# An attention kernel's projections: pieces and their evictions set by a table for each body

## The chip, the cores and the metric

The kernel runs on one core of one Trainium2 chip. The time is that of one launch on the device, in microseconds (us); of several runs the median is given. The core has a matrix engine (TensorE, PE in the rows), VectorE (DVE), ScalarE (ACT), GpSimd (POOL) and SyncE (SP, which here issues transfers). Each runs its own list of instructions in order, and waits at semaphores for the others.

## The reference: what is computed

`x` has 8 images of 56 by 56 cells with 256 channels, in float32. The block is attention between windows, behind a group norm:

```python
x = x + L0_conv_ref(gn(x), ...)            # gn: 32 groups of 8 channels
# inside:
qkv = einsum('nchw,oc->nohw', xc, qkv_w) + qkv_b
q_r, k_r = pool(q), pool(k)                # means over 7 x 7 regions of 8 x 8 cells
_, idx_r = top_k(q_r @ k_r, 4)             # for each region: the 4 regions to look at
attn = softmax(einsum('bhnqd,bhnkd->bhnqk', qs * SCALE, key_g))   # 64 queries, 256 keys, 8 heads
out = einsum('bhnqk,bhnkd->bhnqd', attn, val_g)
out = out + conv3x3_depthwise(v) + lepe_b
out = einsum('nchw,oc->nohw', out, out_w) + out_b
```

So each of the 8 x 49 regions gathers the keys and values of 4 regions of its image, and beside that there are four projections (q, k, v, output) and a 3 x 3 convolution for each channel.

## The kernel before

**Tiles.** A row is a band of 8 lines of cells: 448 cells and 7 regions, and 7 rows make an image, so there are 56 rows. Channels lie on the 128 partitions in two halves, so a projection of one row has two *chunks*, `v0` and `v1`, `k0` and `k1`, and so on, each 128 by 448 in one of two PSUM banks (`chunk_bank`), which the chunks take in turn. A chunk is 4 *pieces*: two halves of 224 cells, each over two halves of the channels. `vt0` and `vt1` turn the values of a row over (one piece each), `rm` makes the means of the regions of an image, and `late` is half of an output projection that is kept for the last image.

**Bodies.** The program is unrolled into some 200 bodies, each for two regions (a *duo*); one body in each image but the last has a single region. With 25 bodies to an image I number them 0 to 24; body 0 is the single one, which ends the image before. In body h TensorE does the scores of duo h (`scores`, L1218), the product of probabilities and values of duo h-1 (`attend`, L1258), turns the reciprocals of the softmax sums (`turn_recips`, L1266), and then four times: some pieces of projections (`fill`), and the turn of two heads' worth of probabilities for each of the two regions (`turn_probs`, L1240, turns 0 to 3). The pieces fill the time in which TensorE would otherwise wait for the softmax.

**The softmax's loop.** The scores of a duo need all exponentials of the one before (they share banks). VectorE takes the maximum of each turn (L959, four instructions), ScalarE the exponential (`exp`, L744, two heads and their sums for each region), and ScalarE copies each turned bank out (`probs_t_out`, L754). There are two buffers of probabilities: the exponentials of turn 2 need turn 0 done, and those of turn 3 turn 1.

**Evictions.** ScalarE takes v, k, q, vt and rm chunks out of their bank (L701, L691, L720, L711, L729); VectorE takes output chunks, adding the input (`out_half`, L944; `late_half`). A chunk can't begin before the chunk two before it is out of the bank. VectorE also does the convolution (`outer_tap`, L846, 16 a row) and the statistics of later rows, in `row_part`, once for each region (*slot*).

**What sets the order.** `step_order` lists the chunks of each row; this list is the same before and after. `fill_plan` cuts it into bodies by weights: a piece weighs 2, a turn of values 3, a piece of `rm` 1; the four fills of a body get about 4, 5, 4 and what is left up to the goal of the slot. Chunks ended in fills 0 and 1 go out on ScalarE behind the exponentials of turn 2, those ended in fills 2 and 3 at the start of the next body, the first of them ahead of the last copy of probabilities and the others behind it. On VectorE an output chunk goes out ahead of the first slot's part (fill 0), between the two slots (fills 1 and 2), or at the start of the next body, ahead of the maxima (fill 3).

**Transfers.** SyncE stores the turned values of each row (`store_values`) and gathers them for each region in four transfers (`select_values`, L441) into 4 slots (`v_sel`); it reads the indices of 7 regions at a time (L404). GpSimd gathers keys, adds the attention's result to the convolution, and issues the transfers of whole rows.

## Time and profile before

| | us |
|---|---|
| median of 3 runs | 1795.88 (1792.58 to 1802.46) |
| the profiled execution | 1792.81 |
| its span, first to last instruction | 1789.8 |
| busy: TensorE | 1636.2 (91%) |
| busy: VectorE | 1530.6 (86%) |
| busy: ScalarE | 1383.9 (77%) |
| busy: GpSimd | 1052.2 (59%) |

A busy share is a mean over the run. The chain of work that ended last goes 61% over TensorE, 11% over VectorE, 9% over ScalarE, and 10% of it is time between instructions with no wait that shows. The ends of matrix instructions are modelled, so a short wait between two groups of them can be hidden in the busy time; the starts are measured, and from one group's start to the next is what the argument uses. The granted clock was 0.996 of full speed over the run.

### The profile page before, as it was taken

What the parts mean: (1) busy time and instruction counts of PE and PEld (TensorE: products, weight loads), DVE (VectorE), ACT (ScalarE), POOL (GpSimd) and SP (SyncE); (2) the same over time, 40 slices, a digit from 0 to 9 for tenths busy, and PEclk for the clock granted to TensorE, in tenths of its full rate; (3) what the DMA queues carried; (4) which work ended last, traced back from release to release, by engine and by line L of the source; (5) the groups of instructions that cost most, each with busy time, mean ns of one, the idle gap of its engine ahead of it and who ended that gap; (6) DMA issues with size and microseconds to landing.
All of it is one profiled execution on the core that took longest, in us unless ns stands there. A gap on an engine that the chain in (4) does not pass through costs nothing.

```text
span 1789.8 us, 73643 instructions
## 1 busy us (share of the span) xinstructions
PE 1636.2 (91%) x26568; PEld 1377.4 (77%) x26568; DVE 1530.6 (86%) x2951; ACT 1383.9 (77%) x4401; POOL 1052.2 (59%) x2548
## 2 busy tenths in 40 slices
PE   5999999999999899899999999899899999999897
PEld 4877777887778777777777788788787878777676
DVE  6589888899889889888888889899898888889895
ACT  2488778888778788788888788788787888877674
POOL 3256556566566565655565566556556666577664
PEclk9999999999999999999999999999999999999998
DMA  5233434343434343344444444434343334366555
GB/s 200 77 97 120 126 103 139 108 149 117 127 113 137 107 149 115 116 123 122 126 119 129 123 126 121 125 107 151 105 127 102 115 103 129 113 203 196 196 185 191
DMA packets 164632, 234.43 MB, mean 131 GB/s; under 512 B 19232, under 2 KB 146912, under 8 KB 164272
## 3 DMA queue, kind: packets, MB, share of 16 engines
q1 hardware_dynamic: 141408, 129.71, 24.7%
q0 software_dynamic: 22864, 100.02, 16.7%
q8 instruction: 214, 3.51, 0.8%
q14 instruction: 146, 1.20, 0.2%
HBM read 166.80 MB, written 62.85 MB: 128 GB/s over the span
## 4 chain that ended last, share of the span: by engine, by line
PE 61%; DVE 11%; issue 10%; ACT 9%; POOL 4%; DMA 2%; SPq 2%; POOLq 1%; ACTq 0%; DVEq 0%
PE chunk_bank L1124 20%; PE pt_bank L1240 10%; PE s_bank L1218 10%; ACT probs L744 7%; PE o_bank L1258 6%; DVE neg_max L959 5%; PE o_bank L1240 4%; PE chunk_bank L1138 3%; DVE lepe L846 2%; PE o_bank L1266 2%; POOL k_sel L502 2%; PE chunk_bank L1166 2%; PE chunk_bank L1151 1%; POOL lepe L514 1%; DMA v_sel<-v_dram 1%
## 5 line engine op out<-in xcount | busy, mean ns | idle before, releaser
L744 ACT ACTIVATE probs<-s_bank,neg_max 128x256 f32<-128x256 f32 x1568 | 734.0, 483 | 240.7 <-DVE neg_max L959 240.7
L502 POOL COPY k_sel<-k_all 128x128 f32 x1568 | 397.1, 302 | 512.4 <-PE s_bank L1218 421.9
L959 DVE TENSOR_REDUCE neg_max<-s_bank 128x2 f32<-128x512 f32 x784 | 486.8, 682 | 161.2 <-PE s_bank L1218 160.6
L846 DVE SCALAR_TENSOR_TENSOR lepe<-v_band,taps,lepe 128x448 f32<-128x448 f32 x896 | 621.3, 743 | 0.0
L1124 PE MATMUL chunk_bank<-xn,wqkv 128*128 128x224 f32 x2544 | 588.9, 357 | 29.0 <-ACT v_stage L711 13.4
L1124 PEld LDWEIGHTS chunk_bank<-xn,wqkv 128*128 128x128 f32 x2544 | 439.7, 192 | 40.9 <-issue 37.2
L754 ACT COPY probs_t<-pt_bank 128x512 f32<-128x512 f32 x611 | 364.5, 597 | 81.8 <-PE pt_bank L1240 79.3
L1240 PE MATMUL pt_bank<-ident,probs 128*128 128x128 f32 x2444 | 375.9, 276 | 22.4 <-ACT probs L744 13.3
L1240 PEld LDWEIGHTS pt_bank<-ident,probs 128*128 128x128 f32 x2444 | 281.4, 141 | 98.7 <-issue 69.4
L514 POOL TENSOR_TENSOR lepe<-o_norm,lepe 128x128 f32<-128x128 f32 x392 | 263.8, 692 | 150.7 <-DVE o_norm L982 147.3
L744 ACT ACTIVATION_READ_ACCUMULATOR probs<-s_bank,neg_max 128x1 f32 x1568 | 332.1, 212 | 0.0
L1258 PEld LDWEIGHTS o_bank<-probs_t,v_sel 128*32 128x32 f32 x12544 | 186.3, 110 | 103.0 <-issue 96.7
L1258 PE MATMUL o_bank<-probs_t,v_sel 128*32 128x64 f32 x12544 | 221.1, 221 | 23.8 <-issue 18.0
L1218 PE MATMUL s_bank<-k_sel,q_all 32*64 32x256 f32 x6272 | 220.9, 387 | 2.6 <-POOL k_sel L502 2.2
L1138 PE MATMUL chunk_bank<-lepe,wout 128*128 128x224 f32 x696 | 162.1, 355 | 14.0 <-POOL lepe L514 10.2
L1218 PEld LDWEIGHTS s_bank<-k_sel,q_all 32*64 32x64 f32 x6272 | 114.9, 131 | 51.4 <-issue 33.7
L1138 PEld LDWEIGHTS chunk_bank<-lepe,wout 128*128 128x128 f32 x696 | 121.0, 190 | 19.2 <-POOL lepe L514 17.3
L754 ACT COPY probs_t<-o_bank 128x512 f32<-128x512 f32 x173 | 106.3, 614 | 8.1 <-PE o_bank L1240 8.1
L1240 PE MATMUL o_bank<-ident,probs 128*128 128x128 f32 x692 | 103.9, 273 | 0.0
L525 POOL TENSOR_SCALAR lepe<-v_band,taps,btap 128x448 f32<-128x448 f32 x112 | 102.7, 917 | 0.0
L1266 PE MATMUL o_bank<-ident,o_norm 128*128 128x128 f32 x392 | 87.1, 302 | 12.0 <-issue 6.4
L563 POOL TENSOR_SCALAR xn<-xn,rstd,shift 128x448 f32<-128x448 f32 x96 | 93.6, 975 | 0.0
(81 smaller groups left out, 1442.6 us busy)
## 6 DMA issues: line engine op xcount, KB each, us to landing
v_sel<-v_dram SPq DMA_DIRECT2D x1568, 64.0 KB
xn<-x_dram POOLq DMA_DIRECT2D x56, 448.0 KB, 4.9
v_dram<-v_stage SPq DMA_DIRECT2D x112, 224.0 KB
resid<-x_dram POOLq DMA_DIRECT2D x31, 448.0 KB, 4.6
out_dram<-resid POOLq DMA_DIRECT2D x31, 448.0 KB, 5.6
spill<-lepe POOLq DMA_DIRECT2D x25, 448.0 KB, 3.6
xn<-spill POOLq DMA_DIRECT2D x25, 448.0 KB, 5.5
resid<-x_dram POOLq DMA_DIRECT2D x25, 224.0 KB, 3.3
```

The lines of the kernel that those rows point to most:

```text
L502: last = pool.tensor_copy(k_sel[:, r % K_SLOTS, :, RT * j:RT * (j + 1)], k_all[:, b % 2, :, bass.ds(reg[j] * RT, RT)])
L514: pool.tensor_tensor(cells, o_norm[:, r - DUOS[h][0], :].rearrange("p (k r c) -> p k r c", k=KC, r=RS), cells, ALU.add).then_inc(o_row_don ...
L744: act.activation(probs[:, 2 * (j % 2) + i, :], s_bank[:, u, KEYS * at:KEYS * (at + 1)], ACT.Exp, bias=neg_max[:, h % 2, col:col + 1], accu ...
L754: act.copy(probs_t[:, j, :], turn_bank(h, j)[:, :]).then_inc(probs_t_evac, 1)
L846: ins = dve.scalar_tensor_tensor(row, v_band[:, n % BANDS, k, t // 3:t // 3 + RS, t % 3:t % 3 + W], taps[:, k, t:t + 1], row, ALU.mult, AL ...
L959: dve.tensor_reduce(neg_max[:, h % 2, 2 * j:2 * j + 2], scored, AX.X, ALU.max, negate=True).then_inc(max_done, 1)
L1124: ins = pe.matmul(bank_of(kind, n, k)[:, cols], wqkv[:, part, col:col + P], xn[:, part, n % X_RING, cols], start=(part == 0), stop=(part = ...
L1138: ins = pe.matmul(bank_of("out", g, m)[:, cols], wout[:, part, P * m:P * (m + 1)], lepe[:, part, g % LEPE_RING, cols], start=(part == 0), ...
L1218: last = pe.matmul(s_bank[RT * k:RT * (k + 1), u, KEYS * i:KEYS * (i + 1)], q_all[s, g % Q_RING, k, rc, :], k_sel[s, r % K_SLOTS, k, :], s ...
L1240: ins = pe.transpose(bank[:, at:at + P], probs[:, 2 * (j % 2) + i, P * c:P * (c + 1)], ident[:])
L1258: last = pe.matmul(o_bank[HD * u:HD * (u + 1), P * i + RT * k:P * i + RT * (k + 1)], v_sel[:, r % V_SLOTS, c, HD * head:HD * (head + 1)], ...
L1266: last = pe.transpose(o_bank[:, P * (DUO + i):P * (DUO + i + 1)], o_norm[:, i, :], ident[:])
```

## The change: a table of pieces and places

For each body of an image a table now holds four counts, the pieces of the four fills, and two strings of four letters, one for ScalarE and one for VectorE: where in its order the engine takes out a chunk that ended in that fill. On ScalarE, 0 is behind the exponentials of turn 1, 1 behind the copy of turn 0, 2 behind the exponentials of turn 2, 3 behind the copy of turn 1, 4 behind the exponentials of turn 3, 5 behind the copy of turn 2, and W at the start of the next body as before. On VectorE, N is ahead of the first slot's part, H behind it, I between two taps of the second slot's part, E at the body's end, and W at the start of the next body. There is one table for the first image, one for the next six, one for the last. Values are stored two regions later: by SyncE behind the gathers of slot 1 of the next row instead of slot 6 of their own (the last row of an image as before).

```diff
-def quotas(h, slots):
-    if not is_duo(h) or not slots:
-        return [0] * (2 * len(slots))
-    return [4, 5, 4, 0] if len(slots) == DUO else [4, 0]
+NEXT_IMAGES = (
+    "3171 .1WW ....", "1404 .2.4 ....", "2322 .1.5 ..H.", "2223 .3.W ....", "2340 .14. ....",
+    "2513 0..W .H.E", "2241 1.WW ....", "2404 .2.W ....", "2422 1W.. ...E", "0114 .2WW ....",
...
+def body_table(h):
+    if h == 0:
+        return [0] * (2 * len(BODIES[0][1])), "", ""
+    firsts = [DUO_OF[NREG * b] + (b < NB - 1) for b in range(NB)]
+    b = max(b for b in range(NB) if firsts[b] <= h)
+    table = FIRST_IMAGE if b == 0 else NEXT_IMAGES if b < NB - 1 else LAST_IMAGE
+    counts, by_act, by_dve = table[h - firsts[b]].split()
+    return [int(c) for c in counts], by_act, by_dve
...
 def fill_plan():
+        for count in body_table(h)[0]:
             place = []
+            for key, i in stream[at:at + count]:
                 if place and place[-1][0] == key:
                     place[-1] = (key, place[-1][1], i + 1)
                 else:
                     place.append((key, i, i + 1))
             places.append(place)
+            at += count
...
+def taken(h, by_act, at):
+    if not 0 <= h < len(PLAN):
+        return []
+    _, act_at, dve_at = body_table(h)
+    return [key for f, place in enumerate(PLAN[h]) for key, _, last in place
+            if last == pieces(key)[0] and (key[0] not in ("out", "late")) == by_act
+            and (act_at if by_act else dve_at)[f] in at]
...
-                    if rc == 0 and rr == 1 and is_row(kv - 1):
+                    if rc == 1 and rr and is_row(kv - 1):
                         store_values(kv - 1)
                     if rc == 1 and rr == LAST and is_row(kv):
                         load_index(kv // NWIN)
-                    if rc == 6 and rr not in (0, LAST) and is_row(kv):
-                        store_values(kv)
...
             for h, slots in BODIES[1:]:
+                left = taken(h - 1, True, "W")
                 for key in left[:1]:
                     chunk_out(*key)
                 if is_duo(h - 1):
                     probs_t_out(h - 1, turns_of(h - 1) - 1)
                 for key in left[1:]:
                     chunk_out(*key)
+                if is_duo(h):
+                    exp(h, 0)
+                    exp(h, 1)
+                    chunks_out(h, "0")
+                    probs_t_out(h, 0)
+                    chunks_out(h, "1")
+                if is_duo(h) and turns_of(h) > 2:
                     exp(h, 2)
+                    chunks_out(h, "2")
                     probs_t_out(h, 1)
+                    chunks_out(h, "3")
                     exp(h, 3)
+                    chunks_out(h, "4")
                     probs_t_out(h, 2)
+                    chunks_out(h, "5")
...
                 if is_duo(h - 1):
                     normalize_o(h - 1)
+                sums_out(h, "N")
+                if len(slots) == 1:
                     row_part(slots[0])
+                    sums_out(h, "HI")
                 else:
+                    row_part(slots[0])
+                    sums_out(h, "H")
+                    row_part(slots[1], h)
+                    for slot in slots[2:]:
+                        row_part(slot)
+                sums_out(h, "E")
```

The first place is ScalarE's order in body 2 of the second image, from the last copy of probabilities of body 1 on; line numbers of the two kernels differ (L744, L754, L691 and L701 of before are L759, L769, L706 and L716 of after). Before:

```order
L754 COPY probs_t<-pt_bank 128x512
L744 ACTIVATE probs,denom<-s_bank,neg_max 128x256 x4
L754 COPY probs_t<-pt_bank 128x512
L744 ACTIVATE probs,denom<-s_bank,neg_max 128x256 x2
L701 ACTIVATE v_band<-chunk_bank,bqkv 128x8x56
L691 ACTIVATE k_all<-chunk_bank,bqkv 128x8x7x8
L754 COPY probs_t<-pt_bank 128x512
L744 ACTIVATE probs,denom<-s_bank,neg_max 128x256 x2
L754 COPY probs_t<-o_bank 128x512
L691 ACTIVATE k_all<-chunk_bank,bqkv 128x8x7x8
```

And the same stretch after:

```order
L769 COPY probs_t<-pt_bank 128x512
L716 ACTIVATE v_band<-chunk_bank,bqkv 128x8x56
L759 ACTIVATE probs,denom<-s_bank,neg_max 128x256 x4
L769 COPY probs_t<-pt_bank 128x512
L759 ACTIVATE probs,denom<-s_bank,neg_max 128x256 x2
L706 ACTIVATE k_all<-chunk_bank,bqkv 128x8x7x8
L769 COPY probs_t<-pt_bank 128x512
L759 ACTIVATE probs,denom<-s_bank,neg_max 128x256 x2
L706 ACTIVATE k_all<-chunk_bank,bqkv 128x8x7x8
L769 COPY probs_t<-o_bank 128x512
```

The eviction of `v1` has moved out of the stretch between the first and the last exponentials to a place ahead of them, that of `k0` has stayed, and that of `k1` goes ahead of the copy of turn 2.

The second place is TensorE's order in body 6 of the second image, from the first piece behind the turned reciprocals to the last turn: the pieces of k (`xn,wqkv`), of the output (`lepe,wout`) and the turn of values (`ident,v_band`). Before:

```order
L1124 MATMUL chunk_bank<-xn,wqkv 128x224
L1138 MATMUL chunk_bank<-lepe,wout 128x224
L1240 MATMUL pt_bank<-ident,probs 128x128 x4
L1138 MATMUL chunk_bank<-lepe,wout 128x224 x3
L1240 MATMUL pt_bank<-ident,probs 128x128 x4
L1138 MATMUL chunk_bank<-lepe,wout 128x224 x2
L1240 MATMUL o_bank<-ident,probs 128x128 x4
L1138 MATMUL chunk_bank<-lepe,wout 128x224 x2
L1166 MATMUL chunk_bank<-ident,v_band 114x128 x4
L1240 MATMUL pt_bank<-ident,probs 128x128 x4
```

And after:

```order
L1144 MATMUL chunk_bank<-xn,wqkv 128x224 x2
L1260 MATMUL pt_bank<-ident,probs 128x128 x4
L1158 MATMUL chunk_bank<-lepe,wout 128x224 x5
L1260 MATMUL pt_bank<-ident,probs 128x128 x4
L1158 MATMUL chunk_bank<-lepe,wout 128x224
L1260 MATMUL o_bank<-ident,probs 128x128 x4
L1158 MATMUL chunk_bank<-lepe,wout 128x224 x2
L1186 MATMUL chunk_bank<-ident,v_band 114x128 x4
L1260 MATMUL pt_bank<-ident,probs 128x128 x4
```

The body has one piece of k more, and the first output chunk now begins and ends between turns 0 and 1, with the first piece of the second output chunk behind it.

The third place is VectorE's order from the first slot's part of that body to the maxima of body 7. Before:

```order
L846 SCALAR_TENSOR_TENSOR lepe<-v_band,taps,lepe 128x448 x2
L944 SCALAR_TENSOR_TENSOR resid<-chunk_bank,bout,resid 128x448
L846 SCALAR_TENSOR_TENSOR lepe<-v_band,taps,lepe 128x448 x3
L965 RECIPROCAL rdenom<-denom 128x8
L972 COPY o_norm<-rdenom 128x256
L944 SCALAR_TENSOR_TENSOR resid<-chunk_bank,bout,resid 128x448
L959 TENSOR_REDUCE neg_max<-s_bank 128x2 x4
```

And after:

```order
L863 SCALAR_TENSOR_TENSOR lepe<-v_band,taps,lepe 128x448 x2
L961 SCALAR_TENSOR_TENSOR resid<-chunk_bank,bout,resid 128x448
L863 SCALAR_TENSOR_TENSOR lepe<-v_band,taps,lepe 128x448 x3
L961 SCALAR_TENSOR_TENSOR resid<-chunk_bank,bout,resid 128x448
L982 RECIPROCAL rdenom<-denom 128x8
L989 COPY o_norm<-rdenom 128x256
L976 TENSOR_REDUCE neg_max<-s_bank 128x2 x4
```

The second eviction has moved ahead of the reciprocals; nothing else has.

## Rows read from the trace of the kernel before

**Rows 1.** The page's first line: the span and the instructions.

```profile
span 1789.8 us, 73643 instructions
```

**Rows 2.** Windows, twelve bodies, an image: us; busy PE, PEld, DVE, ACT, POOL; clock, DMA.

```profile
1146.75:1152.72 5.97, 4.88 (x99) 3.54 (x98) 4.67 (x9) 3.67 (x12) 5.96 (x15) 1.00 0.37 111
727.00:735.62 8.62, 8.22 (x112) 7.09 (x111) 7.53 (x17) 7.06 (x26) 5.18 (x12) 1.00 0.51 165
523.21:532.11 8.90, 8.26 (x135) 7.02 (x134) 7.27 (x14) 7.66 (x25) 4.57 (x12) 1.00 0.37 120
744.52:753.22 8.70, 8.43 (x141) 6.93 (x140) 7.43 (x13) 6.33 (x21) 5.89 (x13) 1.00 0.21 60
644.27:652.19 7.92, 7.83 (x133) 6.54 (x133) 7.27 (x15) 6.75 (x23) 5.42 (x14) 1.00 0.40 127
668.76:676.78 8.02, 8.02 (x136) 6.99 (x135) 6.88 (x13) 6.86 (x23) 5.07 (x12) 1.00 0.40 127
652.19:660.84 8.65, 7.60 (x135) 6.29 (x135) 8.01 (x16) 7.31 (x24) 5.59 (x13) 1.00 0.29 73
676.78:685.74 8.96, 8.32 (x138) 7.07 (x137) 8.19 (x18) 6.54 (x22) 4.76 (x13) 1.00 0.16 49
685.74:694.23 8.49, 7.90 (x135) 6.71 (x134) 7.88 (x15) 7.60 (x24) 5.30 (x13) 1.00 0.47 129
694.23:702.58 8.35, 8.08 (x135) 6.70 (x134) 7.05 (x14) 7.17 (x23) 4.16 (x12) 1.00 0.59 193
702.58:711.43 8.85, 7.97 (x138) 6.42 (x137) 7.95 (x20) 7.30 (x23) 6.42 (x15) 1.00 0.36 113
1138.23:1146.75 8.52, 7.88 (x133) 6.65 (x132) 8.14 (x20) 6.70 (x22) 2.62 (x6) 1.00 0.33 91
933.98:1146.75 212.77, 197.24 (x3290) 165.69 (x3289) 188.25 (x365) 172.06 (x551) 126.94 (x314) 1.00 0.41 124
```

**Rows 3.** Timeline of a body: start, us, engine, line, instructions, [idle before, releaser].

```profile
644.27 1.12 PE L1218 MATMUL s_bank<-k_sel,q_all 32*64 32x256 f32 x32
...
645.50 2.48 DVE L959 TENSOR_REDUCE neg_max<-s_bank 128x2 f32<-128x512 f32 x4 [0.58 <-PE s_bank L1218]
646.23 0.47 ACT L744 ACTIVATE probs<-s_bank,neg_max 128x256 f32<-128x256 f32 x1 [1.17 <-DVE neg_max L959]
...
647.86 1.30 PE L1124 MATMUL chunk_bank<-xn,wqkv 128*128 128x224 f32 x6
...
648.99 0.60 PE L1240 MATMUL pt_bank<-ident,probs 128*128 128x128 f32 x4
...
649.45 0.64 ACT L691 ACTIVATE k_all<-chunk_bank,bqkv 128x448 f32<-128x448 f32 x1
649.97 0.60 ACT L754 COPY probs_t<-pt_bank 128x512 f32<-128x512 f32 x1
...
651.63 0.63 PE L1240 MATMUL pt_bank<-ident,probs 128*128 128x128 f32 x4
```

**Rows 4.** Timeline of body 2, third image: TensorE at the first piece of `k1`.

```profile
529.18 0.99 PE L1124 MATMUL chunk_bank<-xn,wqkv 128*128 128x224 f32 x4 [0.64 <-ACT v_band L701]
```

**Rows 5.** TensorE's waits, whole run: us, times, longest; the second, all from 1566 on.

```profile
PE o_bank L1258 <- issue: 18.0, 19, 2.5
...
PE o_bank L1258 <- DMA v_sel<-v_dram: 5.4, 3, 2.6
```

**Rows 6.** SyncE: timeline of one region's gathers and a store.

```profile
542.73 3.07 SPq L441 DMA_DIRECT2D v_sel<-v_dram  x4
545.90 1.17 SPq L420 DMA_DIRECT2D v_dram<-v_stage  x2
```

**Rows 7.** SyncE in the image from 933.98 to 1146.75: loads of indices (ns); waits.

```profile
L404 SPq TENSOR_LOAD <-idx_row x7: 2159/2164/2316, 958.6 to 1142.6; - x7
SPq L377 <- ACT v_stage L711: 6.2, 4, 3.7
```

**Rows 8.** VectorE's evictions in that image: count, busy us, mean ns, idle before.

```profile
L944 DVE SCALAR_TENSOR_TENSOR resid<-chunk_bank,bout,resid 128x448 f32<-128x448 f32 x10 | 6.8, 675 | 0.0
```

More of the change, by code:

```diff
@@ L166, in pieces @@
     return QUARTERS, 2
-def quotas(h, slots):
-    if not is_duo(h) or not slots:
-        return [0] * (2 * len(slots))
-    return [4, 5, 4, 0] if len(slots) == DUO else [4, 0]
-def fill_plan():
-    order = [(s, [key for key in step_order(s) if is_row(key[1])]) for s in range(STEPS)]
-    load = [sum(pieces(key)[0] * pieces(key)[1] for key in keys) for _, keys in order]
-    stream = [(key, i) for _, keys in order for key in keys for i in range(pieces(key)[0])]
-    at, spent, plan = 0, 0, []
-    for h, slots in BODIES:
-        places = []
-        quota = quotas(h, slots)
-        for f, enough in enumerate(quota):
-            slot = slots[f // 2]
-            if f == len(quota) - 1 or not enough:
-                done = slot + 1 if f % 2 else slot + 0.5
-                goal = sum(load[:int(done // NWIN)]) + (load[int(done // NWIN)] * (done % NWIN) / NWIN
-                                                        if done < STEPS * NWIN else 0)
-            else:
-                goal = spent + enough
-            place = []
-            while at < len(stream):
-                key, i = stream[at]
-                weight = pieces(key)[1]
-                if spent + weight / 2 > goal:
-                    break
@@ new lines, in body_table @@
+def body_table(h):
[6 more added lines that the diff above has]
+    return [int(c) for c in counts], by_act, by_dve
+def fill_plan():
+    stream = [(key, i) for s in range(STEPS) for key in step_order(s) if is_row(key[1]) for i in range(pieces(key)[0])]
+    at, plan = 0, []
+    for h in range(len(BODIES)):
+        places = []
+        for count in body_table(h)[0]:
+            place = []
+            for key, i in stream[at:at + count]:
@@ L789, in _, with chunks_out @@
             q_out(1, 1)
+            def chunks_out(h, at):
+                for kind, n, k in taken(h, True, at):
+                    chunk_out(kind, n, k)
             for h, slots in BODIES[1:]:
-                paired = len(slots) == DUO
-                left = ended(h - 1, 2) + ended(h - 1, 3) if len(BODIES[h - 1][1]) == DUO else ended(h - 1, 1)
+                left = taken(h - 1, True, "W")
                 for key in left[:1]:
@@ L1021, in _, with sums_out @@
             maximum(0, 1)
-            def sums_out(h, f):
-                for kind, n, k in ended(h, f):
+            def sums_out(h, at):
+                for kind, n, k in taken(h, False, at):
                     if kind == "out":
@@ L1040, in row_part @@
                     outer_tap(now, 0)
+                    sums_out(h, "I")
                     outer_tap(now, 1)
@@ L1077, in row_part @@
                     outer_tap(now, 14)
+                    sums_out(h, "I")
                     outer_tap(now, 15)
             for h, slots in BODIES[1:]:
-                paired = len(slots) == DUO
                 if is_duo(h - 1):
```

57 lines of the change are left out of this document (22 added, 35 removed), and 8 rows, old and new, of tables (FIRST_IMAGE, NEXT_IMAGES).

## The prediction

> **What bounds the kernel now.** I read three views in this order: windows cut at the starts of the scores, one a body; the timeline of one body; and the waits of single engines. The page gives a span of 1789.8 us [rows 1], and the profiled execution took 1792.81, so 3.0 us lie around the span; the median of the runs shown, 1795.88, is 3.07 above it.
>
> The windows [rows 2] show in turn bodies 0, 1, 2, 3, one of the kind of 16, one of 19, 17, 20, 21, 22, 23, 24, and a whole image. The reader is to see that no engine is full: in the image TensorE is busy 197.24 of 212.77 us, VectorE 188.25, ScalarE 172.06. Bodies come in kinds that repeat: 7.92 us (bodies 4, 8, 9, 11, 15, 16, 18), 8.02 (5, 12, 19), 8.65 (10, 17), 8.96 (6, 13, 20), 8.49 (7, 14, 21), and 5.97, 8.62, 8.90, 8.70, 8.35, 8.85, 8.52 for 0, 1, 2, 3, 22, 23, 24. With these counts an image takes 207.1 us; the 212.77 of the one shown holds 5.7 more, in which TensorE stands still between its instructions without a wait that the profile explains, most of it at the products with the values: 18.0 us in 19 places over the run [rows 5].
>
> The timeline [rows 3] shows what sets the shortest kind: a loop. Scores begin at 644.27; the first maximum at 645.50 (1.23); the first exponential at 646.23 (0.73); the last turn at 651.63 (5.40), once all exponentials are done; the next scores at 652.19 (0.56; the window's end). Sum 7.92. Inside the 5.40 ScalarE took out one chunk, from 649.45 to 649.97: 0.52. So a body costs 7.40 and 0.52 for each eviction between its first and last exponential; an eviction behind the last one runs beside the turn, the scores and the maximum.
>
> TensorE's own need is the second limit. The body with 8.02 busy of 8.02 has ten pieces, and three pieces took from 647.86 to 648.99, so 0.38 each [rows 2, 3]: nine pieces need 7.64, ten 8.02. VectorE's work is the third: 8.14 in body 24, 8.01 in 17. In body 20 it is 8.19, plus the second output eviction, which falls into the next window (0.68 each [rows 8]), less some 0.3, by estimate, that the window holds of the neighbours' reciprocals and taps: 8.56 from maximum to maximum. A body can't be shorter than the longest of the three.
>
> What is over that is a fourth thing, a wait for a bank. In body 2 the first piece of `k1` starts at 529.18, released by the eviction of `v1` on ScalarE [rows 4], which stands behind the exponentials of turn 2. The row shows 0.64 of it; the rest hides in modelled ends.
>
> **The change, part by part.** Amount of work: none is added, evictions and pieces are the same; all terms are waits. For each kind I take the longest limit after the change.
>
> Bodies 2, 7, 14, 21 and 10 had two evictions inside the exponentials and get one (in 7, 14 and 21 `q0` goes to W, in 10 `vt1`, in 2 `v1` is out earlier): to 7.92 each, but 8.10 for body 2, where the means and `v1` stand with the last copies of body 1 and make the products with the values late, by an estimated 0.2. Gains 0.80, 3 x 0.57, 0.73: 3.24.
> Bodies 6, 13, 20: `k1` leaves ahead of the copy of turn 0, so the second output chunk finds its bank free; VectorE's 8.56 is next. 3 x 0.40 = 1.20.
> Body 17: TensorE's wait for the output bank shrinks, since the second turn of values is moved to fill 2; VectorE's 8.01 and a little give 8.10. 0.55.
> Body 22 has no eviction inside any more: 7.40 by the loop, 7.60 with TensorE's need for eight pieces and its starts. 0.75. Body 23 keeps two: 8.44 by the loop, 8.50. 0.35. Body 24: VectorE's 8.14, 8.20. 0.32. Body 3: to 8.05, TensorE's need. 0.65. Body 1 gets one piece more (0.38) and loses its waits: 0.12. Bodies 5, 12, 19 lose a piece: 8.02 to 7.92, 0.30.
> Losses: 8, 9, 11 get a tenth piece, 3 x 0.12. Bodies 4 and 18 follow bodies in which two evictions stand ahead of the last copy of probabilities, which the products with the values wait for: one more eviction of 0.64 [rows 3], of which I let 0.28 and 0.18 through to the loop. Together 0.82 away.
> Sum: 3.24 + 1.20 + 0.55 + 0.75 + 0.35 + 0.32 + 0.65 + 0.12 + 0.30 - 0.82 = 6.66 us an image. The first image has a table of its own of the same sort and I give it the same: seven images, 46.6 us. All of this stands in the loop, so it moves the end.
>
> The unknown here is how much the third limit and the new places hold back. From above: with every body at 7.92 an image takes 5.97 + 24 x 7.92 = 196.1, a gain of 11.0, 77 us over seven. From below: every output eviction can become such a wait as in body 17, 8.65 against 7.60 busy, 1.05 each with ten an image [rows 8], against the 6.66: a loss of 3.8, 27 us. I take the sum, whose limits are read in bodies of this very kernel, and keep both ends.
>
> The last image has no projections of keys and values; its evictions are few, and two or three of its bodies have an output eviction moved off a body full of VectorE work. I take 2 us, between a loss of 5.4, as much as its waits for gathered values are now [rows 5], and a gain of as much.
>
> Later stores of values: SyncE waited 6.2 us an image for ScalarE there [rows 7], with the next gathers behind it in its queue. Its work in an image is 49 regions at 3.17 (542.73 to 545.90), 7 loads at 2.16 and 7 stores at 1.17 [rows 6, 7]: 178.7 of 206.1, so it stays ahead, and the store has two rows' time until its buffer is written again. The cover for it is the slots for two duos. TensorE's three waits for values, 5.4 us, are all in the last image, where nothing is stored: I take 0, between nothing lost and 6.2 gained an image.
>
> The 18.0 us of unexplained waits I leave as they are.
>
> Sum: 1792.81 - 46.6 - 2 = 1744.2 on the profiled execution's own time, 1747 on the level of the median.
>
> One rule speaks against the change. In the image VectorE and GpSimd are busy 188.25 and 126.94 us of 212.77, so they overlap for at least 102.4 us, and in 206.1 us for at least 109.1 [rows 2]. The Trainium skill, "SBUF — State Buffer", section "Who interferes with whom", says that a VectorE instruction with two inputs in SBUF and a GpSimd instruction that reads SBUF exclude each other for their whole length. By the rows the durations hold and the sum stays; by the rule up to the added 6.7 us of overlap could come back as longer VectorE work.
>
> **The rivals.**
> - VectorE holds more. It stands idle 0.6 to 0.8 us in nearly every body (7.92 - 7.27, 8.65 - 8.01, 8.96 - 8.19, 8.49 - 7.88), 0.4 in body 24. If it needs that idle time, bodies 6, 13, 20, 17, 23 and 24 gain nothing (1.20 + 0.55 + 0.35 + 0.32 = 2.42) and an image gains 4.24: 30 and 2 us, 1764. For it: 188.25 is much of 206. Against: bodies differ, and it idles because the scores come late.
> - More is won: bodies reach the loop's 7.92 all through, 77 us: 1719. For it: the loop is the only limit that all bodies share. Against: ten pieces and the output evictions need more than 7.92.
> - The change doesn't do what it says: a bank that is free earlier only lets TensorE run into the next wait, and the kinds keep their lengths: 1796. For it: TensorE needs only 7.64 of the 7.92 in the shortest kind, so it waits there too. Against: the long kinds have a wait, not work.
> - VectorE's instructions stretch beside GpSimd's by the added overlap, 6.7 us an image, which is the whole gain: 1794. The rule above is the reason to name it. Against: GpSimd's order doesn't change, and the overlap is large already.
> - Slower: output chunks in fill 3 or with the letter E leave late, both banks are held, and TensorE waits 1.05 for each of the ten: 27 us lost, 1823. It decides where VectorE ends such an eviction more than some 2 us after the next scores began: the first exponential starts 1.96 after them [rows 3], and at about that place the first piece of the body wants its bank. In body 6 I expect it about 0.8 us after.
>
> **How the numbers follow.** The forecast 0.52; VectorE 0.18; more 0.10; no effect 0.07; stretch 0.05; slower 0.08. A measurement of this kernel can tell about 0.5%, 9 us, from no change. Faster by more than that: the first three and a little of the two at 1794 and 1796, 0.82; within it 0.10; slower 0.08. The forecast's own range is 1733 to 1761. The range reaches from 1716, just below the best case, to 1790, towards no change.
>
> **What would show it.** Right: scores start every 7.9 to 8.1 us in bodies 2, 7, 10, 14 and 21, and every 8.5 to 8.6 in 6, 13 and 20; TensorE's waits for `chunk_bank` on ScalarE's evictions nearly gone; VectorE's wait for the scores (0.58 in the body shown [rows 3]) gone in 6, 13, 20 and 24; an image near 200 us and unexplained waits. SyncE's wait in the store gone. Wrong: bodies of 8.5 us among the five; a wait of some 1 us on VectorE's evictions in bodies 7, 10, 14 and 21; waits for `v_sel` in the first seven images; taps longer than before.

## The result and the profile after

The changed kernel took 1754.21 us (median of 4 runs, 1752.82 to 1761.20) beside 1799.04 for the kernel before: a ratio of 0.9767, 95% interval 0.9738 to 0.9797. In a second measurement it took 1756.52 (6 runs) beside 1789.39: 0.9805, 0.9765 to 0.9846. By these ratios the change wins 35 to 42 us, where I forecast 49. The profiled execution is the longest of the first four, 1761.2 us.

The page's first line, which answers to [rows 1]:

```profile
span 1759.1 us, 73643 instructions
```

The same windows as [rows 2], of the changed kernel: in turn bodies 0, 1, 2, 3, 6, 7, 10, 13, 17, 18, 20, 22, 23 and a whole image; columns as there.

```profile
913.77:920.13 6.36, 4.88 (x100) 3.54 (x98) 6.29 (x11) 3.71 (x12) 6.36 (x15) 1.00 0.38 111
503.80:512.98 9.18, 8.87 (x115) 7.39 (x113) 7.65 (x17) 6.67 (x23) 5.36 (x13) 1.00 0.50 157
512.98:521.00 8.02, 7.87 (x134) 6.68 (x132) 6.66 (x12) 7.62 (x27) 4.61 (x12) 1.00 0.36 117
521.00:529.69 8.69, 8.42 (x142) 6.93 (x140) 7.97 (x16) 7.40 (x25) 5.91 (x13) 1.00 0.24 63
545.57:554.02 8.45, 8.45 (x140) 7.42 (x138) 7.81 (x16) 6.90 (x23) 4.76 (x13) 1.00 0.19 53
554.02:561.97 7.95, 7.95 (x136) 6.52 (x134) 7.88 (x15) 6.74 (x23) 5.40 (x13) 1.00 0.40 120
578.01:586.04 8.03, 7.19 (x132) 5.78 (x130) 7.88 (x15) 6.79 (x23) 6.08 (x13) 1.00 0.22 63
602.55:611.14 8.59, 8.59 (x140) 7.46 (x138) 7.95 (x16) 6.76 (x23) 4.78 (x13) 1.00 0.19 53
635.06:643.24 8.18, 8.02 (x138) 6.72 (x136) 7.54 (x15) 7.01 (x24) 5.60 (x13) 1.00 0.22 62
643.24:651.45 8.21, 8.11 (x134) 6.59 (x132) 8.11 (x17) 6.95 (x24) 4.81 (x12) 1.00 0.53 161
659.37:667.90 8.53, 8.53 (x140) 7.35 (x138) 7.89 (x16) 6.83 (x23) 4.76 (x13) 1.00 0.19 56
675.99:683.86 7.87, 7.87 (x134) 6.31 (x132) 6.82 (x15) 6.77 (x23) 4.18 (x12) 1.00 0.58 188
683.86:693.07 9.21, 8.49 (x140) 6.84 (x138) 8.35 (x21) 8.12 (x25) 6.34 (x15) 1.00 0.41 127
...
497.44:701.41 203.97, 198.44 (x3291) 164.79 (x3289) 187.62 (x365) 171.22 (x551) 129.00 (x313) 1.00 0.42 129
```

The same work of TensorE (3291 instructions) is done in 203.97 us instead of 212.77; its busy time hardly moves, its idle time falls from 15.5 to 5.5. Not all of that is the change: the image after is the shortest of the six middle ones (203.97 to 212.36), the one before is among the longest (208.20 to 212.97), and their means are 206.7 and 211.4. Undisturbed bodies repeat to a few hundredths from image to image in every kernel here, so I compare kernels by one number: for each body the lower median of its length over the six middle images, summed over the 25. I call it the bodies' sum: 207.14 before, 203.11 after, 4.0 less.

The groups of TensorE's instructions over the run say where that came from (busy, mean ns, and idle time before them with its releasers), after and then before:

```profile
L1144 PE MATMUL chunk_bank<-xn,wqkv 128*128 128x224 f32 x2544 | 577.6, 356 | 7.7 <-issue 4.9 <-DVE xn L899 2.5 <-DVE resid L961 0.2
...
L1278 PE MATMUL o_bank<-probs_t,v_sel 128*32 128x64 f32 x12544 | 221.7, 221 | 27.9 <-issue 19.8 <-DMA v_sel<-v_dram 4.6 <-ACT probs_t L769 2.2
...
L1158 PE MATMUL chunk_bank<-lepe,wout 128*128 128x224 f32 x696 | 157.5, 353 | 0.7 <-issue 0.6
...
L1186 PE MATMUL chunk_bank<-ident,v_band 128*114 128x128 f32 x404 | 60.4, 274 | 5.1 <-DVE resid L961 2.9 <-ACT k_all L706 1.8 <-issue 0.4
```

```profile
L1124 PE MATMUL chunk_bank<-xn,wqkv 128*128 128x224 f32 x2544 | 588.9, 357 | 29.0 <-ACT v_stage L711 13.4 <-ACT k_all L691 4.5 <-ACT v_band L701 4.1
...
L1138 PE MATMUL chunk_bank<-lepe,wout 128*128 128x224 f32 x696 | 162.1, 355 | 14.0 <-POOL lepe L514 10.2 <-ACT k_all L691 3.8
...
L1166 PE MATMUL chunk_bank<-ident,v_band 128*114 128x128 f32 x404 | 60.4, 275 | 20.5 <-DVE resid L944 13.6 <-ACT k_all L691 6.8
```

No wait of a projection's piece for one of ScalarE's evictions is left in the first group or in that of the output; the same three groups of pieces idled 29.0, 14.0 and 20.5 us before, 13.5 together now. The products with the values still stand 19.8 us without a wait that shows, against 18.0 [rows 5]. SyncE's wait in the store fell from 84.6 to 60 us over the run; I had written that it would be gone.

### The profile page after: what moved, and what is told of

Its sections match the earlier page's. It is cut to its first block, busy times and chain, and to the rows that moved or that the text cites. A ratio compares the mean times of both kernels' runs of the same rounds, so it can differ in the third digit from the quotient of the medians.

```text
span 1759.1 us, 73643 instructions
## 1 busy us (share of the span) xinstructions
PE 1643.8 (93%) x26568; PEld 1374.0 (78%) x26568; DVE 1532.4 (87%) x2951; ACT 1380.3 (78%) x4401; POOL 1064.4 (61%) x2548
## 3 DMA queue, kind: packets, MB, share of 16 engines
q1 hardware_dynamic: 141408, 129.71, 25.1%
## 4 chain that ended last, share of the span: by engine, by line
PE 71%; DVE 11%; ACT 6%; issue 6%; DMA 2%; SPq 2%; POOL 1%; POOLq 0%; DVEq 0%; ACTq 0%
PE chunk_bank L1144 22%; PE pt_bank L1260 13%; PE s_bank L1238 11%; PE o_bank L1278 8%; PE chunk_bank L1158 5%; DVE neg_max L976 5%; ACT probs L759 4%; PE o_bank L1260 4%; DVE lepe L863 3%; PE o_bank L1286 3%; PE chunk_bank L1186 2%; PE chunk_bank L1171 2%; DMA v_sel<-v_dram 1%; SPq L458 1%; ACT probs_t L769 1%
## 5 line engine op out<-in xcount | busy, mean ns | idle before, releaser
L759 ACT ACTIVATE probs<-s_bank,neg_max 128x256 f32<-128x256 f32 x1568 | 733.3, 482 | 232.4 <-DVE neg_max L976 232.4
L517 POOL COPY k_sel<-k_all 128x128 f32 x1568 | 403.4, 305 | 469.3 <-PE s_bank L1238 385.2
L1144 PE MATMUL chunk_bank<-xn,wqkv 128*128 128x224 f32 x2544 | 577.6, 356 | 7.7 <-issue 4.9
L769 ACT COPY probs_t<-pt_bank 128x512 f32<-128x512 f32 x611 | 366.0, 599 | 52.3 <-PE pt_bank L1260 51.3
L1260 PE MATMUL pt_bank<-ident,probs 128*128 128x128 f32 x2444 | 380.1, 278 | 28.5 <-ACT probs L759 16.0
L1260 PEld LDWEIGHTS pt_bank<-ident,probs 128*128 128x128 f32 x2444 | 276.6, 141 | 123.1 <-issue 71.6
L529 POOL TENSOR_TENSOR lepe<-o_norm,lepe 128x128 f32<-128x128 f32 x392 | 268.3, 704 | 147.9 <-DVE o_norm L999 144.5
L759 ACT ACTIVATION_READ_ACCUMULATOR probs<-s_bank,neg_max 128x1 f32 x1568 | 331.7, 212 | 0.0
L1278 PE MATMUL o_bank<-probs_t,v_sel 128*32 128x64 f32 x12544 | 221.7, 221 | 27.9 <-issue 19.8
L1158 PE MATMUL chunk_bank<-lepe,wout 128*128 128x224 f32 x696 | 157.5, 353 | 0.7 <-issue 0.6
L769 ACT COPY probs_t<-o_bank 128x512 f32<-128x512 f32 x173 | 105.7, 611 | 9.8 <-PE o_bank L1260 8.9
L1260 PEld LDWEIGHTS o_bank<-ident,probs 128*128 128x128 f32 x692 | 82.7, 141 | 14.5 <-issue 8.0
```

The lines of the kernel that those rows point to most:

```text
L517: last = pool.tensor_copy(k_sel[:, r % K_SLOTS, :, RT * j:RT * (j + 1)], k_all[:, b % 2, :, bass.ds(reg[j] * RT, RT)])
L529: pool.tensor_tensor(cells, o_norm[:, r - DUOS[h][0], :].rearrange("p (k r c) -> p k r c", k=KC, r=RS), cells, ALU.add).then_inc(o_row_don ...
L759: act.activation(probs[:, 2 * (j % 2) + i, :], s_bank[:, u, KEYS * at:KEYS * (at + 1)], ACT.Exp, bias=neg_max[:, h % 2, col:col + 1], accu ...
L769: act.copy(probs_t[:, j, :], turn_bank(h, j)[:, :]).then_inc(probs_t_evac, 1)
L1144: ins = pe.matmul(bank_of(kind, n, k)[:, cols], wqkv[:, part, col:col + P], xn[:, part, n % X_RING, cols], start=(part == 0), stop=(part = ...
L1158: ins = pe.matmul(bank_of("out", g, m)[:, cols], wout[:, part, P * m:P * (m + 1)], lepe[:, part, g % LEPE_RING, cols], start=(part == 0), ...
```

## The experiments

All ratios are to the kernel before, measured beside each run, with the 95% interval. Every kernel of this section has the later stores, unless the text says otherwise. **Stores alone.** The kernel before, with

```
-                    if rc == 0 and rr == 1 and is_row(kv - 1):
+                    if rc == 1 and rr and is_row(kv - 1):
                         store_values(kv - 1)
-                    if rc == 6 and rr not in (0, LAST) and is_row(kv):
-                        store_values(kv)
```

> The kernel before with the later stores of values and nothing else. My theory (the gain is made in the softmax's loop and at the banks, the stores are idle time of SyncE alone): within 4 us of before, 1796 +- 4, with SyncE's waits on v_stage down from 84.6 to about 60 us and TensorE's unexplained standstills at about 18 us. Rival (the stores free the gathers, and the gain beyond the regular bodies, some 18 of 45 us, comes from there): about 1778.

Measured: 1786.32, 0.9972 (0.9950 to 0.9995). The bodies' sum is 207.13, every body as before. So the later stores win about 5 us (by the interval 1 to 9), outside the bodies; I had counted them at nothing. The two traces don't say how: their six middle images are equally long (1268.5 and 1268.3 us), and the difference stands in the last image (214.3 and 208.3).

**Counts alone, places alone, the middle images alone.** The counts alone stand in all images, the other two in the six middle ones. Of the new places only those could go with the old counts whose chunk ends in the same body in both tables. The entry that decided the first two, that of body 17:

```
 before              2222 .2.W N...
 after               2214 .245 .N..
 counts alone        2214 .2WW .H..
 places alone        2222 .4.5 N...
```

> The new counts of pieces with the old places (ScalarE behind the exponentials of turn 2 or at the next body's start; VectorE ahead of slot 1, between the slots, or at the next body's start), and the later stores. My theory: counts alone win little, since the second eviction stays inside the exponentials: bodies 7, 14 and 21 stay at 8.5, bodies 6, 13 and 20 at 8.8 to 9.0, an image within 2 us of before; 1785 to 1798. Rival (the work is better spread, and the places only follow): two thirds of the gain, about 1766.

> The old counts of pieces with the new places in the six middle images, for chunks that end in the same body in both tables and where the letter can stand (25 fills to an image); first and last image as before; later stores. My theory: bodies 7, 14, 21 and 10 go from 8.49 and 8.65 to 8.0 and 8.1 (0.45 x 3 + 0.6), bodies 6, 13, 20 from 8.96 to 8.6 (0.36 x 3), body 2 from 8.90 to 8.3: about 3.5 us an image over six images, 21 us, 1775. Rival (places win only where the counts make the bank free in time): under 1 us an image, 1790 or more.

> The new table in the six middle images alone, the first and the last image with the old counts and places; later stores. My theory: 3.9 us an image by the bodies (207.06 to 203.1), 24 us, and some of the irregular standstills with it: 1766 to 1773. Rival (the first and the last image bring the part of the gain that the bodies don't explain, about 18 us): 1772 here, and most of the rest with the ends alone; rival (irregular standstills fall everywhere because of the later stores): 1755 to 1760.

Measured: counts alone 1801.30, 1.0046 (1.0018 to 1.0073); places alone 1801.07, 1.0051 (1.0029 to 1.0074); both in the middle images 1756.08, 0.9792 (0.9745 to 0.9839). Each half alone is slower than before, and my theory missed both. The bodies' sums are 210.62, 210.73 and 203.03, and body 17 explains it: 11.83 and 12.68 us instead of 8.65. The timeline of that body with the counts alone, 1086.78 to 1097.14:

```profile
1091.19 2.27 DVE L862 SCALAR_TENSOR_TENSOR lepe<-v_band,taps,lepe 128x448 f32<-128x448 f32 x3
...
1093.38 0.67 DVE L960 SCALAR_TENSOR_TENSOR resid<-chunk_bank,bout,resid 128x448 f32<-128x448 f32 x1
...
1094.20 0.62 PE L1185 MATMUL chunk_bank<-ident,v_band 128*114 128x128 f32 x4 [2.34 <-DVE resid L960]
...
1095.29 0.59 ACT L768 COPY probs_t<-o_bank 128x512 f32<-128x512 f32 x1 [1.33 <-PE o_bank L1259]
```

VectorE takes the output chunk out only behind three taps, the second turn of values waits 2.34 for that bank, and the last-but-one turn of probabilities stands behind it in TensorE's order. The table's N puts the eviction ahead of the taps. With the places alone the bank was held by ScalarE (the letter 4 is behind the exponentials of turn 3), for 2.16 us. This is the kind of wait of the slower case that I gave 0.08, late evictions that hold the banks, at twice its price, and the changed kernel avoids it by one letter.

The clock then adds to it. Windows of body 17 in the third image of the first kernel, and in the fourth of the second:

```profile
660.00:662.00 2.00, 0.39 (x4) 0.42 (x5) 2.00 (x5) 1.37 (x5) 2.00 (x3) 1.00 0.30 82
662.00:664.00 2.00, 2.00 (x13) 1.90 (x11) 1.66 (x5) 1.07 (x2) 0.01 (x1) 0.75 0.69 217
664.00:666.00 2.00, 2.00 (x8) 1.47 (x6) 0.00 (x0) 0.00 (x0) 0.00 (x0) 0.50 0.35 130
```

```profile
871.00:873.00 2.00, 0.24 (x1) 0.27 (x2) 2.00 (x4) 2.00 (x7) 0.82 (x2) 1.00 0.59 116
873.00:875.00 2.00, 2.00 (x9) 1.78 (x9) 0.93 (x3) 0.10 (x1) 0.00 (x0) 0.53 0.65 242
```

Behind a stretch with 0.39 or 0.24 us of matrix work in 2.00, the granted clock goes from 1.00 to about 0.50, the lower of its two levels, 1.2 GHz. With the counts alone two of six images kept the full clock through the same wait: body 17 was 10.36 there and 11.8 to 12.0 in the four others.

The middle images alone took 10 us less than I expected (1766 to 1773), although the bodies' sum came out as expected. The rest shows as fewer standstills of TensorE (what each body takes over its median comes to 20.3 us over the middle images, 26.5 before and 26.4 with the stores alone) and a shorter last image (210.7 against 214.3), for which I have no cause. And this kernel, with the old table in the first and the last image, is as fast as the whole change (0.9792 beside 0.9767 and 0.9805): the two other tables add nothing that the time can tell.

**The same two without the bad places.**

```
 counts alone, body 17:      2214 .2WW .H..  ->  2214 .2WW .N..
 places alone, body 17:      2222 .4.5 N...  ->  2222 .2.5 N...
 places alone, bodies 14, 21, 22, 0: ScalarE's letters as before
```

> The new counts of pieces with the old places in the six middle images, except that in body 17 the output chunk goes out ahead of the first slot's part (N) as in the new table, so that the standstill of 2.3 us which the run with the counts alone had there is gone; first and last image as before; later stores. In that run an image's bodies came to 210.6 us, 11.8 of them in body 17. My theory: body 17 falls to 8.2 to 8.7, an image to 207.0 to 207.4, as before, and the time is 5 us under before for the later stores: 1785 to 1790. Rival (another chunk takes over the wait in body 17 or 18, since counts and places only fit together): 209 us an image or more, no faster than before.

> The old counts with new places in the six middle images, without those that made things worse in the first run of this kind: bodies 14, 21, 22 and 0 keep their old letters on ScalarE, and in body 17 the turned values go out behind the exponentials of turn 2. First and last image as before; later stores. My theory (an eviction out of the exponentials wins by itself where the bank's next user comes late enough): bodies 6, 13, 20 at 8.2 to 8.4, 7 at 8.17, 24 at 7.9, 17 at 8.65, an image at 204.3; 17 us by the bodies and 5 by the stores, 1770 to 1775. Rival (only counts and places together win, as e4 against e2 and e3 seemed to say): 1785 or more.

Measured: counts 1778.08, 0.9935 (0.9915 to 0.9955), places 1772.92, 0.9905 (0.9882 to 0.9929). The windows of bodies 6 and 17 with the counts:

```profile
552.81:562.33 9.52, 8.73 (x139) 7.46 (x138) 8.85 (x19) 7.34 (x24) 4.75 (x13) 1.00 0.18 50
645.30:653.48 8.18, 8.02 (x137) 6.73 (x136) 7.54 (x15) 6.99 (x23) 5.59 (x13) 1.00 0.21 65
```

and of bodies 6 and 20 with the places:

```profile
553.80:562.16 8.36, 8.30 (x137) 6.97 (x136) 7.54 (x16) 6.71 (x23) 4.75 (x13) 1.00 0.17 50
672.10:680.25 8.15, 8.15 (x137) 6.90 (x136) 7.41 (x16) 6.71 (x23) 4.75 (x13) 1.00 0.19 56
```

One letter takes body 17 from 11.83 to 8.18. The bodies' sums are 207.14 for the counts, nothing won, as expected, and 205.59 for the places, 1.55 won where I expected 2.8. Together they win 4.0; that isn't quite the sum of two halves, since not all of the new places could be tried with the old counts. The counts win 0.4 to 0.9 in each of bodies 2, 10, 17 and 21 and lose 0.3 to 0.6 in 1, 6, 9, 13 and 18; the places win in 6, 7, 13, 20 and 24 and lose in 0, 4, 14 and 21. Both at once keep most gains and take away most losses: body 6 is 8.46 instead of 9.52 with the counts, body 9 is 8.02 instead of 8.52, body 14 is 8.09 instead of 8.51 and 8.84. The counts' time is 7 us lower than bodies and stores explain; I find that in fewer standstills (19.6 us against 26.5 over the middle images) and a shorter last image in its trace (209.2 against 214.3), and have no cause for it.

With the places, bodies 14, 21 and 0 stayed at 8.84, 8.83 and 6.43 although they had their old letters back, so their own letters aren't the cause. Measured from the first maximum of a body to that of the next, they take 8.65, 8.46 and 4.99 (8.50, 8.50 and 5.08 before): all of the loss in 21 and 0, and half of it in 14, is VectorE's work for the body ahead, which now ends sooner than VectorE does.

**Mending the bodies that my forecast missed; the last image.** Two entries of the middle images, and in the second kernel also the old table for the last image:

```
 body 22:  2222 .W.5 ....  ->  2222 .2.W ....
 body 0:   22 .1 ..        ->  22 .W ..
```

> The changed kernel once more, so that the next ones are compared with it on one chip: 1754 +- 4, a ratio to before of 0.977.

> The changed kernel with two entries of the table of the six middle images changed: in body 22 the chunks v0 and v1 go out behind the exponentials of turn 2 and at the next body's start instead of both ahead of the last copy of probabilities, and in the single body q1 goes out at the next body's start instead of inside the exponentials. My theory (my forecast missed bodies 23 and 0 for these two places): body 23 from 9.21 to 8.5 us, body 0 from 6.36 to 5.97, body 22 from 7.87 to at most 7.95; 1.0 us an image, 6 us, 0.35% under the changed kernel. Rival (VectorE's work sets bodies 23 and 0, as my forecast's second case had it): no change, within 1 us.

> As the one before, and the last image with its old counts and places. My theory (the profiles of the changed kernel and of the kernel with the new table in the middle images alone have 219.3 and 210.7 us for the last image, and 207.6 and 215.5 for the first, and the two kernels' ratios to before stand only 0.25% apart): the new table loses about 3.5 us in the last image, so 3.5 us under the kernel before this one in this call. Rival (the last image's excess in that profile was one of its irregular standstills, and its table gains the 2 us that I forecast): 2 us over it.

Measured, in this order: 1756.52, 0.9805; 1754.72, 0.9798 (0.9758 to 0.9839); 1754.28, 0.9793 (0.9752 to 0.9834). Nothing won that can be told, and my theory fell in two of three bodies. Body 23 went from 9.21 to 8.84 (I had named 8.5), but body 22 from 7.87 to 8.35, and body 0 stayed at 6.34. Bodies 22 and 23 of this kernel, and ScalarE and TensorE in a body 22:

```profile
674.94:683.30 8.36, 7.85 (x135) 6.25 (x132) 7.32 (x17) 7.30 (x24) 4.17 (x12) 1.00 0.62 196
683.30:692.14 8.84, 8.42 (x141) 6.82 (x138) 7.95 (x20) 7.64 (x24) 6.26 (x15) 1.00 0.39 125
```

```profile
893.02 0.64 ACT L715 ACTIVATE v_band<-chunk_bank,bqkv 128x448 f32<-128x448 f32 x1
...
893.54 0.60 ACT L768 COPY probs_t<-pt_bank 128x512 f32<-128x512 f32 x1
...
894.19 0.66 PE L1259 MATMUL pt_bank<-ident,probs 128*128 128x128 f32 x4 [0.50 <-ACT probs_t L768]
```

Turn 2 goes into `pt_bank` here and waits for the copy of turn 1, which stands behind the eviction of `v0`. The kernel has it in a line that I had not weighed:

```
            return o_bank if j == 2 and not image_work(h) else pt_bank
```

In bodies with means or scores of an image (3, 22, 23) `o_bank` is taken by these, all four turns use one bank, and each copy stands in the loop. Body 22 is then 7.87 without an eviction inside and 8.35 with one; body 23 with two is 8.84: steps of 0.48, on a base 0.47 over my 7.40. The base is read from this order; no run gives these bodies a second bank.

The last image's old table makes 0.4 us. In the traces the last image is 208.0 to 214.3 us with the old table (seven kernels) and 213.2 to 219.3 with the new (six), but the kernel made to test the old one shows 213.4: no gain of 2 us, and whether it loses any stays open.

**VectorE's places, and body 22 once more.**

```
 bodies 6, 9, 20:  E -> W      body 13:  I -> H
 body 22:  2222 .W.5 ....  ->  2222 .3.W ....
```

> The changed kernel with two edits in the middle images that touch different bodies. VectorE's letters E and I back to W and H in four bodies (5, 8, 12, 19 of the table, seen in bodies 6, 9, 13 and 20): my theory is that the work from maximum to maximum is the same, and bodies 6, 13 and 20 stay at 8.46 to 8.6; rival (the place E is what brought them under 8.96): 8.8 to 9.0 in these three, 1.2 us an image. And in body 22 the chunk v0 goes out behind the copy of turn 1 and v1 at the next body's start: the timeline of the kernel with v0 behind the exponentials of turn 2 has turn 2 released by the copy of turn 1, which stood behind that eviction, so with the eviction behind the copy body 22 should be 7.95 instead of 8.35, and body 23 8.84; an image 0.3 us shorter, which the time can't show; rival: body 22 stays at 8.3. Time 1752 to 1757.

Measured: 1756.98, 0.9816 (0.9797 to 0.9835). Bodies 6, 13, 20 stay at 8.46, 8.58, 8.53: of VectorE's new letters the N of body 17 matters, and a little the I of body 13, without which body 14 is 8.32 instead of 8.09. Body 22:

```profile
674.42:682.75 8.33, 8.10 (x134) 6.26 (x133) 7.26 (x17) 7.61 (x24) 4.16 (x12) 1.00 0.59 200
```

My 7.95 was wrong, the rival right: behind the copy of turn 1 the eviction delays the next exponentials instead, by the same amount.

**The stores again.** The changed kernel with its stores at the old place (the first experiment's diff turned round), and with each store made twice (2 and 3 write the same bands to a copy that nobody reads):

```
-                for h in range(2):
+                for h in range(4):
```

> The changed kernel with the stores of values where they were. The later stores alone, on the kernel before, gave a ratio of 0.9972, 5 us, with the same bodies (207.1 us an image in both). My theory: the same 5 us are lost here, 0.25 to 0.35% over the changed kernel, with the bodies' lengths as in the changed kernel and SyncE's waits on v_stage at some 85 us. Rival (in the new order the evictions of values come at other times, and the early store costs nothing, as I forecast for before): within 1 us of the changed kernel.

> The changed kernel with each store of values made twice, the second time to a copy that nobody reads (25.7 MB more, on SyncE's queue). Bodies should keep their lengths in all theories. With the stores at their early place the irregular standstills of TensorE over the six middle images rose from 23.8 to 35.0 us, and one of 4.6 us ended just after an instruction packet had landed that itself came late. Theory (transfers on the same engines hold up the packets of instructions): doubled stores bring back some 10 us of standstills, 1762 to 1770. Rival (it was SyncE's own wait at the early place, which pushed the gathers together behind it): within 3 us of the changed kernel.

Measured: early 1764.01, 0.9834 (0.9789 to 0.9879), 7.5 us over the changed kernel by their medians; its runs spread from 1753 to 1767, and the profiled one is the slowest. Doubled 1756.61, 0.9817 (0.9780 to 0.9854), level with the changed kernel. The bodies' sums are 202.99 in both. With early stores the standstills over the middle images (each body's length over its median) come to 35.0 us, with doubled ones to 25.1, against 23.0 and 23.8 in the changed kernel's two traces; but the kernel before has 26.5 and 26.4, with early stores and with later ones. Two places hold nearly all of the difference: body 22 of the fifth image (6.7 us over its median, 1.5 in the changed kernel) and body 8 of the seventh (6.4 and 1.3). TensorE in the first, with the early stores, and then in the changed kernel's second trace:

```profile
1095.88 1.10 PE L1280 MATMUL o_bank<-probs_t,v_sel 128*32 128x64 f32 x64
1101.53 0.69 PE L1288 MATMUL o_bank<-ident,o_norm 128*128 128x128 f32 x2 [4.55 <-issue]
```

```profile
1097.22 0.44 PE L1286 MATMUL o_bank<-ident,o_norm 128*128 128x128 f32 x2 [1.54 <-issue]
```

So it isn't the stored bytes. Nor is it that SyncE runs late: with doubled stores its spare time, the wait for a free slot, fell from 143.1 us to 47.5, and nothing followed:

```profile
SPq L458 <- PE o_bank L1278: 143.1, 107, 15.4
...
SPq L458 <- PE o_bank L1278: 47.5, 31, 10.0
```

What is left of the causes that I can name is when the store falls among the other transfers; no run here changes that alone, so it stays open.

## Why the prediction was right, and where it was not

- The loop of 7.40 and 0.52 for each eviction: right in the five bodies that lose one. Forecast 7.92 (8.10 for body 2), measured 8.02, 7.97, 8.09, 8.09 and 8.03 for bodies 2, 7, 14, 21, 10. Gains of 0.4 to 0.9 each, 2.85 against 3.24. From first maximum to first maximum, which leaves out what the body ahead hands on, they take 8.02, 7.88, 8.02, 8.02 and 8.03.
- Bodies 6, 13, 20 to 8.56: 8.46, 8.59, 8.53, and for the reason that was given. The 8.56 was worked out from maximum to maximum; measured so, the bodies take 8.52, 8.65 and 8.60 (8.96 before). VectorE goes on without a wait into the next body's maxima, where it waited for the scores before. The first maximum of body 7 before, of body 7 after, and of body 21 with the places alone:

```profile
566.93 2.48 DVE L959 TENSOR_REDUCE neg_max<-s_bank 128x2 f32<-128x512 f32 x4 [0.36 <-PE s_bank L1218]
```

```profile
552.61 1.86 DVE L863 SCALAR_TENSOR_TENSOR lepe<-v_band,taps,lepe 128x448 f32<-128x448 f32 x3
...
555.42 1.28 DVE L976 TENSOR_REDUCE neg_max<-s_bank 128x2 f32<-128x512 f32 x2
```

```profile
681.87 1.28 DVE L975 TENSOR_REDUCE neg_max<-s_bank 128x2 f32<-128x512 f32 x2
```

  With the places alone the next scores come sooner, after 8.36, 8.36 and 8.17, but the next first maximum then comes 1.53, 1.39 and 1.59 behind them instead of 1.23, and from maximum to maximum it is 8.66, 8.55 and 8.55. In the changed kernel TensorE is full as well: the windows show it busy for the whole body.
- TensorE's need of 0.38 a piece: bodies 8, 9, 11 at 8.02 (8.04), 5, 12, 19 at 7.92, as said. Body 17 8.18 (8.10), 18 8.21 (8.10), 4 7.95 (8.20), 24 8.02 (8.20). Body 18 has its length for another reason than the one given: VectorE's work of body 17, 8.48 from maximum to maximum, puts its first maximum 1.52 behind its scores, and from there it takes 7.91.
- The step that failed is the sum's terms for four bodies, 2.4 of the 2.6 us an image by which the sum of 6.66 was too large. In two of them, 23 and 0, each body was held against its limits alone, and VectorE's work runs over into the next. *Body 23, "keeps two: 8.44 by the loop, 8.50"*: 9.21. One bank for all turns makes it 8.84, the same as before. In the other 0.37 two things come together. Two evictions stand ahead of the last copy:

```profile
683.63 1.16 ACT L716 ACTIVATE v_band<-chunk_bank,bqkv 128x448 f32<-128x448 f32 x2 [0.38 <-PE chunk_bank L1144]
684.68 0.59 ACT L769 COPY probs_t<-pt_bank 128x512 f32<-128x512 f32 x1
```

  The products with the values wait 0.44 for that copy and start at 685.52. I had priced that effect in bodies 4 and 18 and not here. And VectorE, whose work for body 22 now runs into body 23, begins the maxima 1.60 behind the scores of 683.96, without a wait:

```profile
685.56 2.48 DVE L976 TENSOR_REDUCE neg_max<-s_bank 128x2 f32<-128x512 f32 x4
```

  In the kernel that has body 22 at 8.35 again, this is 1.23. The first turn starts 1.17 behind the first exponential in both kernels, so VectorE's 0.37 is enough by itself; no run parts the two. Bodies 22 and 23 together go from 17.19 to 17.08. *Body 3, "to 8.05"*: stays at 8.70; it is such a body too (turn 2 waits for its copy), though what else holds it I didn't test. *Body 1, one piece more and no waits*: 9.18, half a microsecond longer than before (the counts alone have it too, 9.25, the places alone don't, 8.62), since fill 1 has a single piece, turn 1 waits for a copy, and seven pieces come behind it. *Body 0 unchanged*: 6.36 for 5.97. Body 24 ends half a microsecond sooner, but VectorE isn't ready:

```profile
913.15 2.66 DVE L863 SCALAR_TENSOR_TENSOR lepe<-v_band,taps,lepe 128x448 f32<-128x448 f32 x3
915.73 0.19 DVE L982 RECIPROCAL rdenom<-denom 128x8 f32<-128x8 f32 x1
```

  Its taps run into body 0, and TensorE waits 0.64 for the reciprocals, against 0.29 before:

```profile
916.60 0.44 PE L1286 MATMUL o_bank<-ident,o_norm 128*128 128x128 f32 x2 [0.64 <-DVE o_norm L989]
```

```profile
936.32 0.44 PE L1266 MATMUL o_bank<-ident,o_norm 128*128 128x128 f32 x2 [0.29 <-DVE o_norm L972]
```

  These three taps take 2.66 us with GpSimd at work beside them all the time; the three at 552.61 above, beside which GpSimd is idle but for the first 0.1 us, take 1.86. Bodies 24 and 0 together go from 14.49 to 14.38. That is the rival "VectorE holds more": of the six bodies that it named, 17, 23 and 24 are where most of a gain, in the body itself or the one ahead, went back to VectorE (17 and 18 together go from 16.57 to 16.39).
- First image, taken to gain the same 6.66: 214.06 to 207.56, 6.5. Last image, 2: not seen.
- Stores, taken at 0 in bounds of 0 to 6.2 an image: about 5 us over the run.
- In sum: six images at 4.0, the first at 6.5 and the stores at 5 make 36 us, inside the measured 35 to 42. But the middle images and the stores alone, 29 of these, win 37 when run by themselves, so the first image's 6.5 doesn't show in the time, and about 8 us there have no cause that I know. That the forecast came close is in part luck: the stores, taken at nothing, gave back a third of what four bodies lacked.
- VectorE's instructions beside GpSimd's: GpSimd's busy time is 129.00 in 203.97 against 126.94 in 212.77, and a tap takes 744 ns in the mean, against 743 before. The mean hides that taps do stretch, in both kernels alike: without a GpSimd instruction beside them they take 672 ns (317 taps before, 293 after), and of those with one beside them for over nine tenths of their length half take more than 800 ns (178 of 348, 192 of 361). The Trainium skill ("SBUF — State Buffer", "Who interferes with whom") says that a VectorE instruction with two inputs in SBUF contends with a GpSimd instruction that reads SBUF; the trace agrees. What failed of this rival is its price: by their instructions both engines work at once for 1021 us of the run before and 1040 after, 19 more and not 6.7 an image.

```profile
L863 DVE SCALAR_TENSOR_TENSOR lepe<-v_band,taps,lepe 128x448 f32<-128x448 f32 x896 | 621.6, 744 | 0.0
```

- The case of late output evictions was real: it needs the counts without the N of body 17, and costs 3 to 4 us there.

## What to carry to other kernels

How much work stands between two waits and where a bank is emptied are one decision: here each alone cost 0.5% with one or two bad letters in it and won 0.65 and 0.95% without them, 0.3 of each by the later stores, and together they won 2%. When a loop is read off one kind of step, look which steps use their buffers in another way (here one bank for all turns), and price those from their own rows. A step that ends sooner hands its time to the next engine in line, so add neighbours in pairs, and measure a body from VectorE's first maximum to the next as well as from scores to scores.

## What was unexpected of the hardware

TensorE's standstills without a wait come mostly at the same instructions, whatever the time: in body 22 of the fifth image 2.29 us before, 0.65 with later stores, 1.54 after and 4.55 with early stores; in body 4 of the fourth image 1.8 to 2.9 in all fourteen traces. Packets of 16 KB on the instruction queue come every 8.2 us (214 in the span). Of the changed kernel's 24 standstills of 0.4 us or more 22 end 1.2 to 1.7 us after such a packet has landed, however long they are; over the fourteen traces it is 267 of 289. In the longest with early stores the packet itself is late: it starts at 1099.13, 2.15 us into the standstill, takes 0.96, and TensorE goes on 1.44 after it has landed. I take it for a wait for instructions; no run here takes the packets away, so it is argued, not shown. The Trainium skill ("Runtime: NRT & Kernel Launch", "Instruction fetch mechanics") calls the cost of such a block mostly hidden. This case's traces agree for nine packets in ten, behind which no such standstill shows; the others cost up to 4.55 us each, and 18 to 36 us a run. The long ones cost twice: behind the 4.55 us the granted clock is 0.50.

```profile
1099.00:1101.00 2.00, 0.00 (x0) 0.00 (x0) 0.00 (x0) 0.00 (x0) 0.00 (x0) 0.65 0.90 256
1101.00:1103.00 2.00, 1.47 (x5) 1.40 (x6) 0.71 (x2) 0.00 (x0) 0.00 (x0) 0.50 0.37 125
```
